# Weights loaded in four groups in the order of their use, and split on VectorE in three places of the first images

## The reference

```python
p = patches(x)                                    # 64 x 196 x 768
h = layernorm(layernorm(p) @ W + b)               # with gains and biases; 192 wide
h = concat([cls, h])                              # 197 tokens
# attention 1: 12 heads of 64
q, k, v = split(ln(h) @ w_qkv.T)                  # q and k then normalised over the heads
h = h + softmax(q @ k.T / scale[head]) @ v @ w_out.T + b_out
# attention 2: 12 heads of 16; q, k, v get a low-rank delta of the 2 best of 8 experts per token
xf = ln(h)
combine = top2(softmax(xf @ Wg.T + bg))
delta = (einsum((xf @ A + ba) * combine, Bm) + combine @ bb) * 2
q, k, v = split(xf @ Wqkv.T + bqkv + delta)
h = h + softmax(q @ k.T / 4) @ v @ Wproj.T + bproj
```

## Time and profile before

| | |
|---|---|
| median of 3 runs | 3148.75 us (3148.18 to 3150.78) |
| profiled execution | 3151.46 us, span in the trace 3148.9 us, granted TensorE clock 0.987 |
| busy | PE 2966.1, DVE 2325.7, ACT 1963.3, POOL 589.9 us |
| one image in the steady part | 47.0 us |
| setup (first DVE operation to `emb_b`) | 36.62 to 59.8 us |

### The profile page before, as it was taken

How to read it: one execution, slowest core, us unless ns; L and a number is a source line. 1 busy time by engine, 2 the same in 40 slices (tenths; PEclk the granted TensorE clock), 3 DMA queues, 4 the chain that set the end, 5 groups by cost and what they waited for, 6 DMA issues and landing times.

```text
span 3148.9 us, 98362 instructions
## 1 busy us (share of the span) xinstructions
PE 2966.1 (94%) x41624; PEld 2429.8 (77%) x41624; DVE 2325.7 (74%) x5441; ACT 1963.3 (62%) x3777; POOL 589.9 (19%) x859
## 2 busy tenths in 40 slices
PE   1799999999999999999999999999999999999996
PEld 1687787787787787887877878778778778778775
DVE  3577777777777777777777777777777777777773
ACT  0466666666666666666666666666666666666663
POOL 1112121111121111211211211211211211211210
PEclk8899999999999999999999999999999999999998
DMA  4000000000000000000000000000000000000000
GB/s 106 17 12 21 12 21 21 12 21 21 13 20 21 14 18 22 19 14 21 22 11 21 21 12 21 21 12 21 21 12 21 21 12 21 22 12 21 14 4 7
DMA packets 28389, 61.26 MB, mean 19 GB/s; under 512 B 4211, under 2 KB 18390, under 8 KB 27959
## 3 DMA queue, kind: packets, MB, share of 16 engines
q1 hardware_dynamic: 27958, 54.98, 5.8%
HBM read 45.29 MB, written 9.68 MB: 17 GB/s over the span
## 4 chain that ended last, share of the span: by engine, by line
PE 58%; DVE 35%; ACT 3%; issue 3%; SPq 1%; DMA 0%; POOL 0%; DVEq 0%; ACTq 0%
PE psum L659 9%; DVE mx L1049 8%; PE psum L668 8%; PE psum L568 8%; PE psum L585 7%; PE psum L595 4%; PE psum L695 3%; PE psum L647 3%; PE psum L629 3%; DVE st L952 3%; DVE mx L1062 2%; PE psum L698 2%; DVE kl L1141 2%; PE psum L705 2%; DVE o_t L1158 2%
## 5 line engine op out<-in xcount | busy, mean ns | idle before, releaser
L820 ACT ACTIVATE ebufs<-psum 99x788 f32<-99x788 f32 x768 | 591.9, 823 | 59.0 <-PE psum L647 45.5
L504 POOL TENSOR_TENSOR veps<-mv,eps_ln 99x2 f32<-99x2 f32 x256 | 116.0, 453 | 2258.9 <-DVE mv L978 1337.4
L1062 DVE TENSOR_REDUCE mx<-psum 99x4 f32<-99x788 f32 x384 | 357.4, 973 | 137.6 <-PE psum L612 137.4
L1049 DVE TENSOR_REDUCE mx<-psum 99x4 f32<-99x788 f32 x384 | 362.7, 973 | 52.5 <-PE psum L604 52.5
L585 PE MATMUL psum<-hn_s,qk_w 128*128 128x197 f16 x3840 | 354.7, 249 | 10.2 <-DVE hn_s L1018 2.9
L585 PEld LDWEIGHTS psum<-hn_s,qk_w 128*128 128x128 f16 x3840 | 322.6, 98 | 31.0 <-DVE kl L1141 19.2
L659 PE MATMUL psum<-ebufs,vx 98*32 98x197 f32 (+1 forms) x6144 | 293.2, 330 | 0.0
L568 PE MATMUL psum<-emb_w,xb 128*99 128x193 f32 x1536 | 267.1, 330 | 16.1 <-DVE emb_b L945 16.1
L568 PEld LDWEIGHTS psum<-emb_w,xb 128*99 128x99 f32 x1536 | 251.2, 168 | 18.4 <-DVE emb_b L945 16.4
L668 PE MATMUL psum<-out_w,qk 128*99 128x192 f32 x1536 | 263.8, 328 | 0.1
L668 PEld LDWEIGHTS psum<-out_w,qk 128*99 128x99 f32 x1536 | 245.1, 166 | 0.3 <-issue 0.3
(11 more groups left out here) (172 smaller groups left out, 6640.0 us busy)
## 6 DMA issues: line engine op xcount, KB each, us to landing
xb<-x_t SPq DMA_DIRECT2D x64, 591.0 KB, 3.8
out<-h SPq DMA_DIRECT2D x128, 73.5 KB
out<-h SPq DMA_DIRECT2D x64, 0.8 KB
vx<-w_qk SPq DMA_DIRECT2D x2, 384.0 KB
qk_sq<-w_emb SPq DMA_DIRECT2D x1, 576.0 KB
out_w<-w_out SPq DMA_DIRECT2D x8, 72.0 KB
vx<-w_qk SPq DMA_DIRECT2D x1, 576.0 KB
qk<-w_lora_b SPq DMA_DIRECT2D x1, 480.0 KB
```

The costliest lines, as they stand in the source:

```text
L504: nc.gpsimd.tensor_tensor(veps[part][s][:], mv[part][s][:, :, 1], eps_ln[:], ALU.add).then_inc(veps_made[1], 1)
L820: nc.scalar.activation(ebuf[n].rearrange("p e a t -> p e (a t)"), psum[0:TR, b + 2 * half:b + 2 * half + 2, 0:2 * NT], ACT.Exp).then_inc(r ...
L1049: nc.vector.tensor_reduce(mx[s][:, :, 2 * i:2 * i + 2].rearrange("p a e -> p e a"), psum[0:TR, b:b + 2, 0:2 * NT].rearrange("p e (a t) -> ...
L1062: nc.vector.tensor_reduce(mx2[s][:, :, at:at + 2].rearrange("p a e -> p e a"), psum[0:TR, b + 2 * half:b + 2 * half + 2, 0:2 * NT].rearran ...
```

## The change

Four semaphores stand in place of one. SP issues, in this order: w_emb and ln1, the first image, the rest of what the embedding needs (`emb_loads`), then what attention 1's q,k need (`qk_loads`), then w_v (`v_loads`), the second image, and then everything else with `consts_loaded` as before. DVE's setup is only the embedding's. The q,k weights are split at the begin of the "start" pass (`weights_of_scores`), v's at the begin of the "first" pass (`weights_of_values`), and attention 2's in the first pass behind the maxima of image 0 (`weights_of_attention2`). PE waits for `setup_dve` at 3, 4 and 5 ahead of the first QK, V and OP. w_qkv2 lands in the q,k tiles of attention 2 (which become one tensor, `qk2`), no longer in `qk[0]`; ACT waits ahead of image 1's QK until the raw weights in `qk[1]` are used up. PE's two setup products change places, and the one that needs no scaled weights no longer waits for them. The splits themselves are the same instructions with the same shapes, so the parts of `weights_of_attention2` that are left out below are as before.

```diff
--- before.py
+++ after.py
-        qh2, ql2 = two("qh2", [128, 2, NTP], F16), two("ql2", [128, 2, NTP], F16)
-        kh2, kl2 = two("kh2", [128, G2, NTP], F16), two("kl2", [128, G2, NTP], F16)
+        qk2 = sb("qk2", [128, 2, 4 + 2 * G2, NTP], F16)
+        qh2, ql2 = [qk2[:, s, 0:2, :] for s in range(2)], [qk2[:, s, 2:4, :] for s in range(2)]
+        kh2, kl2 = [qk2[:, s, 4:4 + G2, :] for s in range(2)], [qk2[:, s, 4 + G2:, :] for s in range(2)]
         neg_t2 = two("neg_t2", [128, NTP], F16)
         sel2_raw, sel2 = sb("sel2_raw", [128, G2, 1]), sb("sel2", [128, G2, TR], F16)
...
         v_raw = ebufs[:].rearrange("p n e a t -> p (n e a t)")[:, 0:2 * INNER].rearrange("p (c f) -> p c f", c=2)
-        qkv2_raw = flat(qk[0], 128, 0, 2, QKV2_RAW)
+        qkv2_raw = qk2[:].rearrange("p s m t -> p (s m t)").bitcast(F32)[:, 0:2 * QKV2_RAW].rearrange(
+            "p (c f) -> p c f", c=2)
         lorab_raw = flat(qk[1], 128, 0, 1, QKV2_RAW)
         bias2_all = flat(qk[1], 128, QKV2_RAW, 1, QKV2_RAW)
...
         consts_loaded = sem("consts_loaded")
...
-        loads = [(emb_raw, w_emb), (ln1_sb, ln1), (ln1b_raw, ln1_bias), (tokc, tok_const), (tok_b, tok_bias),
-                 (lorab_raw, w_lora_b),
-                 (proj_w[:, 2:3, :], w_proj[:, 2:3, :]), (scale_sb, scale), (rowc, row_const),
-                 (mats_sb, mats), (sel_raw[0:64], head_rows[64:128]), (sel_raw[64:128], head_rows[64:128])]
+
+        emb_loads = [(emb_raw, w_emb), (ln1_sb, ln1), (ln1b_raw, ln1_bias), (mats_sb, mats), (tok_b, tok_bias),
+                     (tokc, tok_const), (rowc, row_const)]
+        qk_loads = [(scale_sb, scale), (sel_raw[0:64], head_rows[64:128]), (sel_raw[64:128], head_rows[64:128])]
+        v_loads, loads = [], [(lorab_raw, w_lora_b), (proj_w[:, 2:3, :], w_proj[:, 2:3, :])]
         for j in range(4):
             for c in range(2):
...
                 loads.append((proj_w[32 * j:32 * j + 32, u:u + 1, :], w_proj[32 * r:32 * r + 32, g:g + 1, :]))
-        for raw, w in ((qk_raw, w_qk), (v_raw, w_v), (qkv2_raw, w_qkv2)):
-            loads += [(raw[0:HC, 0:1, :], w[:, 0:1, :]), (raw[HC:128, 0:1, :], w[0:128 - HC, 1:2, :]),
+        for group, raw, w in ((qk_loads, qk_raw, w_qk), (v_loads, v_raw, w_v), (loads, qkv2_raw, w_qkv2)):
+            group += [(raw[0:HC, 0:1, :], w[:, 0:1, :]), (raw[HC:128, 0:1, :], w[0:128 - HC, 1:2, :]),
                       (raw[0:64, 1:2, :], w[128 - HC:HC, 1:2, :]), (raw[64:128, 1:2, :], w[128 - HC:HC, 1:2, :])]
...
         def _(sp):
-            for dst, src in loads:
-                sp.dma_start(dst[tuple(slice(None) for _ in src.shape)], src).then_inc(consts_loaded, 16)
-            sp.wait_ge(bias_cleared, 2)
-            for dst, src in bias_loads:
-                sp.dma_start(dst, src).then_inc(consts_loaded, 16)
+            def load_group(group, loaded):
+                for dst, src in group:
...
-                load(0, s)
+            load_group(emb_loads[0:2], emb_loaded)
+            load(0, 0)
+            load_group(emb_loads[2:], emb_loaded)
+            load_group(qk_loads, qk_loaded)
+            load_group(v_loads, v_loaded)
+            load(0, 1)
+            load_group(loads, consts_loaded)
+            sp.wait_ge(bias_cleared, 2)
+            load_group(bias_loads, consts_loaded)
             passes(sp, body)
             for s in range(2):
...
         def _(pe):
 
-            pe.wait_ge(consts_loaded, 16 * (len(loads) + len(bias_loads)))
+            pe.wait_ge(emb_loaded, 16 * len(emb_loads))
+            for c in range(KC):
+                nc.tensor.matmul(psum[0:TR, 1, 0:D], ln1b_raw[:, c, :], emb_raw[:, c, :],
+                                 start=(c == 0), stop=(c == KC - 1))
             pe.wait_ge(fills, NFILLS)
             pe.wait_ge(setup_dve, 1)
             for c in range(KC):
-                nc.tensor.matmul(psum[0:TR, 0, 0:D], ones, emb_w[:, c, 0:D],
-                                 start=(c == 0), stop=(c == KC - 1))
-            for c in range(KC):
-                mm = nc.tensor.matmul(psum[0:TR, 1, 0:D], ln1b_raw[:, c, :], emb_raw[:, c, :],
+                mm = nc.tensor.matmul(psum[0:TR, 0, 0:D], ones, emb_w[:, c, 0:D],
                                       start=(c == 0), stop=(c == KC - 1))
             mm.then_inc(setup_pe, 1)
             pe.wait_ge(setup_dve, 2)
...
+                    if now.which == "first" and s == 0:
+
+                        if kind == "QK" and i == 0:
+                            pe.wait_ge(setup_dve, 3)
+                        elif kind == "V" and i == 0:
+                            pe.wait_ge(setup_dve, 4)
+                        elif kind == "OP":
+                            pe.wait_ge(setup_dve, 5)
...
-            act.wait_ge(consts_loaded, 16 * (len(loads) + len(bias_loads)))
             act.wait_ge(fills, NFILLS)
             act.wait_ge(setup_dve, 2)
...
                     elif kind == "QK":
+                        if now.which == "first" and s == 1 and i == 0:
+                            act.wait_ge(setup_dve, 5)
                         wait(act, now, pe_sig[kind], p)
...
-            dve.wait_ge(consts_loaded, 16 * (len(loads) + len(bias_loads)))
+            dve.wait_ge(emb_loaded, 16 * len(emb_loads))
             dve.wait_ge(fills, NFILLS)
             nc.vector.tensor_tensor(emb_w[:, :, 0:D], emb_raw,
                                     ln1_sb[:].unsqueeze(2).broadcast_to([128, KC, D]), ALU.mult
                                     ).then_inc(setup_dve, 1)
-
-            nc.vector.tensor_scalar(scale_sb[:], scale_sb[:], WS, None, ALU.mult).then_inc(setup_w, 1)
-            dve.wait_ge(setup_w, 1)
-            nc.vector.reciprocal(inv_scale[:], scale_sb[:])
-            nc.vector.memset(gl_w[64:128, 1:2, :], 0.0)
-            nc.vector.tensor_copy(sel2[:], sel2_raw[:].broadcast_to([128, G2, TR]))
-            for u in range(2):
-                nc.vector.tensor_tensor(kmask[:, u:u + 1], masks[:, u:u + 1], masks[:, u + 2:u + 3], ALU.add
-                                        ).then_inc(setup_w, 1)
-            dve.wait_ge(setup_w, 3)
-            nc.vector.tensor_scalar(kmask[:], kmask[:], 1 / WS, None, ALU.mult)
-            nc.vector.tensor_copy(head_sel[:], sel_raw.broadcast_to([128, H, TR]))
+            dve.wait_ge(setup_pe, 1)
+            nc.vector.tensor_copy(emb_cs[:], psum[0:TR, 0, 0:D])
+            nc.vector.tensor_tensor(emb_b[:], tok_b[:, 0, :], psum[0:TR, 1, 0:D], ALU.add
+                                    ).then_inc(setup_dve, 1)
+            dve.wait_ge(setup_dve, 2)
...
+            splits = [0]
+
+            def split_packed(w, raw):
                 split_weights(lambda v: w[:, v], raw[:, 0])
                 nc.vector.tensor_scalar(w[:, 2], raw[:, 1], WS, None, ALU.mult).then_inc(setup_w, 1)
                 splits[0] += 1
                 dve.wait_ge(setup_w, splits[0])
-                nc.vector.scalar_tensor_tensor(out=w[64:128, 2], in0=raw[64:128, 1], scalar=WS, in1=w[64:128, 2],
-                                               op0=ALU.mult, op1=ALU.subtract)
+                return nc.vector.scalar_tensor_tensor(out=w[64:128, 2], in0=raw[64:128, 1], scalar=WS,
+                                                      in1=w[64:128, 2], op0=ALU.mult, op1=ALU.subtract)
...
-            dve.wait_ge(setup_pe, 1)
-            nc.vector.tensor_copy(emb_cs[:], psum[0:TR, 0, 0:D])
-            nc.vector.tensor_tensor(emb_b[:], tok_b[:, 0, :], psum[0:TR, 1, 0:D], ALU.add
-                                    ).then_inc(setup_dve, 1)
-            dve.wait_ge(setup_dve, 2)
+                nc.vector.reciprocal(inv_scale[:], scale_sb[:])
+                nc.vector.tensor_copy(head_sel[:], sel_raw.broadcast_to([128, H, TR])
+                                      ).then_inc(setup_dve, 1)
+
+            def weights_of_values():
+                dve.wait_ge(v_loaded, 16 * len(v_loads))
+                a = split_packed(v_w, v_raw)
+                a.then_inc(setup_dve, 1)
+
+            def weights_of_attention2():
+                dve.wait_ge(consts_loaded, 16 * (len(loads) + len(bias_loads)))
+                nc.vector.memset(gl_w[64:128, 1:2, :], 0.0)
+                nc.vector.tensor_copy(sel2[:], sel2_raw[:].broadcast_to([128, G2, TR]))
+                for u in range(2):
+                    nc.vector.tensor_tensor(kmask[:, u:u + 1], masks[:, u:u + 1], masks[:, u + 2:u + 3], ALU.add
+                                            ).then_inc(setup_w, 1)
+                splits[0] += 2
+                dve.wait_ge(setup_w, splits[0])
+                nc.vector.tensor_scalar(kmask[:], kmask[:], 1 / WS, None, ALU.mult)
+                split_blocks(qkv2_w[:, 0], qkv2_w[:, 1], qkv2_raw[:, 0])
...
+                split_blocks(lorab_w[:, 0], lorab_w[:, 1], lorab_raw[:, 0], WS * LORA_SCALE)
+                nc.vector.tensor_scalar(bias2_raw, bias2_raw, WS * LORA_SCALE, None, ALU.mult).then_inc(setup_w, 1)
+                splits[0] += 1
```

(61 more changed lines are left out.)

12 lines of the change are left out of this document (6 added, 6 removed).

## The result

| | before | after |
|---|---|---|
| median | 3149.77 us (3148.18 to 3151.2, 4 runs) | 3129.75 us (3129.18 to 3130.24, 4 runs) |
| ratio | | 0.9934, 95% interval 0.9922 to 0.9945 |
| profiled execution | 3151.46, span 3148.9 | 3129.87, span 3128.1 |

The change gains 20.0 us by the medians (0.66%, and the interval is clear of 1) and 20.8 of span between the two profiled executions; 23.75 were forecast. The time lies in the forecast range of 3118 to 3132, 4.75 above the likeliest value.

What follows compares the result with a forecast made beforehand. The prediction held that PE bounds the steady part and a serial chain the start; 36.6 - 11.25 - 1.6 = 23.75 us gained gave 3127.7 profiled, 3125.0 as a median (chance 0.50), range 3118 to 3132.

Steps and rivals of the forecast that it cites:

- first group landed: Start of the kernel: the loads the embedding needs release DVE at 12.0 us instead of 36.6.
- q,k group landed: Start pass: attention 1's q,k weights, 1.58 MB queued behind the first group, are landed at 19.0 us.
- shift there: Image 0's first q,k product starts at 41.5 us against 78.12, which is 36.6 earlier.
- block behind SM.5: Attention 2's splits on DVE after image 0's last maximum: 11.6 us, less 0.33 of slack, cost 11.25.
- Part 4: First pass: v's split delays DVE's T1 by 1.2 us, POOL beside it by 1.5; first q,k product at 41.5.
- The ports (parts 3 and 4): POOL working beside DVE's splits delays DVE by 2.0 us in the start pass and 1.5 in the first pass.
- The rival of no cost at all: DVE's splits beside POOL in the start and first passes lose nothing: 3121.5 us, chance 0.08.
- Full blocking: DVE and POOL block each other in full during the splits, 2.5 + 3.0 us: 3127.0 us, chance 0.18.
- The clock (part 5): After some 11 us idle, PE runs image 1's q,k products at half clock, costing 1.6 us.
- landing out of order: Load groups share the queue, so q,k's group lands at 24 instead of 19: 3130.0 us, chance 0.15.
- hidden: Attention 2's splits behind SM.5 are covered by PE's work and cost nothing: 3112 us, chance 0.05.
- slower by qk2's new addresses: PE reads attention 2's q,k tiles more slowly from the joined tensor, in every image: 3162 us, chance 0.04.

Runs made afterwards that it cites:

- e12: The changed kernel run once more, unchanged, for a second trace; median 3130.49 us, ratio 0.9929 to the kernel before.
- e1: The changed kernel without 35 of attention 2's weight splits behind SM.5 (those weights stay zero); median 3119.95 us, ratio 0.9902 to before.
- e7: The changed kernel with 35 of attention 2's weight splits behind SM.5 run twice in a row; median 3136.75 us, ratio 0.9954 to before.
- e10: The changed kernel with v's split and all of attention 2's weight preparation spread over DVE's gaps, none behind SM.5; median 3112.88 us, ratio 0.9877 to before.
- e6: The changed kernel plus 60 useless PE matmuls ahead of image 1's transposes (T1); median 3128.87 us, ratio 0.993 to before.
- e3: The changed kernel without POOL's three adds of squares for the first two images (row sums set to 1); median 3126.5 us, ratio 0.9921 to before.
- e2: The changed kernel with all weight splits back in the setup, keeping the new load order and groups; median 3135.72 us, ratio 0.995 to before.

## Why the prediction was right or wrong

| step | forecast | measured |
|---|---|---|
| first group landed | 12.0 | 12.08 (9.67 to 15.64 over all traces) |
| setup's end | 18.55 | 18.25 (17.91 + 0.34) |
| q,k group landed | 19.0 | 19.43 |
| DVE's EMB | 27.55 | 27.63 |
| first q,k product | 41.5 | 42.12 |
| shift there | 36.6 | 36.0 |
| block behind SM.5 | 11.6, costs 11.25 | 11.62, costs 36.0 - 24.87 = 11.13 |
| hidden of it | 0.33 | 0.67 (tokens 11.80 later: 108.17 - 72.16 less 114.57 - 90.36) |
| clock | 1.6 | 9.81 - 7.54 = 2.27; 1.64 in e12 |
| steady part | 0 | 0.02 |
| end | 0 | 2.06; 1.3 in e12 |

Sum of the first pair of traces: 36.0 - 11.13 - 2.27 - 2.06 = 20.5; the span shows 20.8.

**Right:** the chain. Every link that the trace of before could show came out within 0.6 us: the landing, both serial pieces on DVE, and the slack, taken as 0.33, that left the block of attention 2 uncovered. e1 and e7 show that last one from two sides, and e10 fits. That the landing was met to 0.1 is in part luck: the same loads landed between 9.67 and 15.64 in eleven traces, with 12.4 in the middle. (Part 4 adds from 36.2 where its own chain gives 36.3; that is 0.1.)

**The ports (parts 3 and 4), a mis-sized term:** taken 2.0 + 1.5 = 3.5, measured 1.80 + 2.14 = 3.94. The start pass was nearly met; in the first pass b_out's add cost 0.69 and the X adds 1.45, within the bound of 3.0 but 0.64 above what was taken. Together that is 0.44 of the missing time; q,k's landing made 0.43 more of it, and small steps gave some of both back. The rival of no cost at all is out. Full blocking, in both directions, is the mechanism that the rows show, but not its price of 5.5: an add that started ahead of DVE's instruction costs DVE only what is left of it. The one of b_out had run for 0.43 when v's second operation came (36.39 and 36.82).

**The clock (part 5), mis-sized in the first trace, with half of the reason:** I took 1.6 because the long idle time ahead of the products looked like that of image 0. The clock was indeed at 0.50 behind it. But the long gap isn't needed: e6 fills it and pays the same, as the clock then falls in the 2.40 us behind T1, which the forecast didn't name. And the price isn't a number but a spread: over the 21 first products (both first images, thirteen traces) that ran at half clock, the way to the squares took between 8.84 and 9.81, against 7.54 to 7.60 at full clock, so 1.3 to 2.3. In the eight of image 1 the clock came back 2.7 (e3) to 6.0 us (after) behind the first product, and the way is longest where it came back last. The first trace was at the upper end, 0.67 over the forecast; e12's 1.64 was met.

**The end, a step that the sum didn't have:** I held the end for unchanged because its instructions are. It lost 2.06 in the one trace and 1.3 in the other to the clock. This is the largest part of the 2.95 us of span that were missing (0.6 at the first product, -0.12 in the block, 0.67 clock, 2.06 end, and 0.26 the other way: 0.18 of that between the squares of image 1 and the begin of the end, within the spread of that part, the rest behind the last token sum and in rounding). With the short end this execution would have been near 3127.8.

**From span to median:** I took the profiled execution of before as 2.7 above its median. By the four runs measured with the kernel after it was 1.7 above (3151.46 against 3149.77), and that of after stands at its median. So the forecast of the median owed 1 us to a single execution.

**The rival whose number was met** is landing out of order, 3130.0, but not its mechanism: q,k's group released DVE at 19.43 and not at 24. Where it came at 22.46 and 23.34 (e2, e10), past the 22 that the forecast had named as a sign of being wrong, the first group was 2.4 and 3.6 later too; the distance between the two was 6.8 to 8.4 in the seven traces in which DVE waited for the second (in the other four it was still in the setup). A time that fits a rival proves nothing until its mark in the trace is looked up. The other two, hidden and slower by qk2's new addresses, are out: the block cost 11.13, and the stretches of 47.0 us have PE busy for 45.88 as before.
